# Attention and token mixing, one core: shift rows by VectorE's transposition and DRAM, and the next group's loads behind the rows of unit 2

## The reference

```
xn = layernorm(x)
q, k, v = heads(xn @ w_in.T)                  # 16 heads of 16 channels
att = where(causal, q @ k.T / 4, 0.0)         # masked scores are 0, not minus infinity
att = softmax(att)                            # so every later key has weight exp(0 - max)
a = (att @ v) @ w_out.T
x_prev = xn, one token later
r = sigmoid((mu_r * xn + (1 - mu_r) * x_prev) @ W_r.T)
k2 = square(relu((mu_k * xn + (1 - mu_k) * x_prev) @ W_k.T))
out = x + a + r * (k2 @ W_v.T)
```

## Time and profile before

| | us |
|---|---|
| median of 3 runs | 1128.43 |
| lowest, highest | 1125.78, 1129.91 |
| profiled execution, its time | 1134.35 |
| profiled execution, its span | 1132.6 |
| TensorE busy | 1080.0 (95%) |
| VectorE busy | 842.5 (74%) |
| ScalarE busy | 713.4 (63%) |
| GpSimd busy | 385.8 (34%) |
| mean granted clock of TensorE | 0.983 of full |

### The profile page before, as it was taken

How to read it: one execution, slowest core, us unless ns; L and a number is a source line. 1 busy time by engine, 2 the same in 40 slices (tenths; PEclk the granted TensorE clock), 3 DMA queues, 4 the chain that set the end, 5 groups by cost and what they waited for, 6 DMA issues and landing times.

```text
span 1132.6 us, 21906 instructions
## 1 busy us (share of the span) xinstructions
PE 1080.0 (95%) x8192; PEld 542.6 (48%) x8192; DVE 842.5 (74%) x1153; ACT 713.4 (63%) x1519; POOL 385.8 (34%) x945
## 2 busy tenths in 40 slices
PE   5999998999999999999989999999999989999998
PEld 3665554544444444444435444444444434444445
DVE  5567787678879787987867878878887878789213
ACT  2433333267776677777757776777777657767672
POOL 3211121354414341444224424442532433244301
PEclk9999999999999899999969999999999989999999
DMA  3585744392019000900280019002800460002033
GB/s 127 174 271 177 214 149 149 131 117 62 2 20 122 30 3 17 124 31 7 37 119 11 6 22 140 8 7 38 124 6 6 58 104 7 6 2 86 25 98 117
DMA packets 53390, 83.61 MB, mean 74 GB/s; under 512 B 6308, under 2 KB 36260, under 8 KB 49572
## 3 DMA queue, kind: packets, MB, share of 16 engines
q1 hardware_dynamic: 52132, 78.01, 32.9%
q0 software_dynamic: 1152, 4.19, 1.2%
HBM read 43.78 MB, written 33.55 MB: 68 GB/s over the span
## 4 chain that ended last, share of the span: by engine, by line
PE 75%; DVE 13%; ACT 4%; issue 4%; DMA 2%; POOL 0%; SPq 0%; ACTq 0%; DVEq 0%; POOLq 0%
PE ps_o L1189 22%; PE ps_s L1175 21%; DVE part_max L347 10%; PE ps_m L330 7%; PE ps_vr L733 4%; ACT probs L1039 4%; PE ps_qk L724 4%; PE ps_m L1220 3%; PE ps_o L1200 2%; PE ps_m L337 2%; PE ps_xt L782 2%; PE ps_qk L733 2%; PE ps_s L1164 2%; DMA x_in<-x 1%; PE ps_pieces L330 1%
## 5 line engine op out<-in xcount | busy, mean ns | idle before, releaser
L1039 ACT ACTIVATE probs<-ps_s 128x512 f32<-128x512 f32 (+3 forms) x1280 | 599.6, 536 | 249.6 <-PE ps_s L1175 241.5
L347 DVE TENSOR_REDUCE part_max<-ps_m 128x2 f32<-128x1024 f32 (+2 forms) x594 | 616.6, 1059 | 152.7 <-PE ps_m L330 115.1
L1175 PE MATMUL ps_s<-q_op,k_op 50*128 50x512 f32 (+3 forms) x1280 | 447.9, 429 | 10.0 <-ACT probs L1039 5.2
L330 PE MATMUL ps_m<-k_op,q_op 48*128 48x512 f32 (+3 forms) x1188 | 355.3, 419 | 16.6 <-DVE part_max L347 9.4
L1175 PEld LDWEIGHTS ps_s<-q_op,k_op 50*128 50x128 f32 x1280 | 210.7, 188 | 313.1 <-ACT probs L1039 214.2
L984 POOL TENSOR_SCALAR_AFFINE_SELECT probs<-probs 128x128 f32<-128x128 f32 x512 | 145.0, 292 | 485.7 <-ACT probs L1039 477.2
L1189 PE MATMUL ps_o<-probs,v_sb 128*32 128x512 f32 (+3 forms) x2560 | 307.9, 551 | 2.2 <-issue 2.2
L330 PEld LDWEIGHTS ps_m<-k_op,q_op 48*128 48x128 f32 x1188 | 169.3, 189 | 43.8 <-DVE part_max L347 33.8
L950 POOL TENSOR_TENSOR diag_weight<-ident,masked_weight 128x256 f32<-128x256 f32 x256 | 150.5, 623 | 40.7 <-ACT masked_weight L1005 40.7
L337 PE MATMUL ps_m<-mask,pick 64*128 64x64 bf16 (+1 forms) x932 | 96.5, 210 | 0.0
L1189 PEld LDWEIGHTS ps_o<-probs,v_sb 128*32 128x32 f32 x2560 | 51.1, 108 | 76.7 <-issue 38.1
(11 more groups left out here) (81 smaller groups left out, 715.9 us busy)
## 6 DMA issues: line engine op xcount, KB each, us to landing
parts_d<-parts SPq DMA_DIRECT2D x32, 512.0 KB, 4.7
q_op<-parts_d SPq DMA_DIRECT2D x42, 256.0 KB, 13.9
k_op<-parts_d SPq DMA_DIRECT2D x42, 256.0 KB, 16.2
vpad_d<-v_pad SPq DMA_DIRECT2D x32, 256.0 KB, 3.3
v_sb<-vpad_d SPq DMA_DIRECT2D x8, 1024.0 KB, 12.4
x_in<-x SPq DMA_DIRECT2D x8, 512.0 KB, 5.2
ffn_d<-ffn SPq DMA_DIRECT2D x8, 512.0 KB, 3.2
attn_t<-normed SPq DMA_DIRECT2D x128, 32.0 KB, 2.0
```

The costliest lines, as they stand in the source:

```text
L330: last = pe.matmul(ps_m[:, f % ring * 2 + e, 0:width], self.q_op[rows, p, j, q0:q0 + P], self.k_op[rows, p, j, pc * CH:pc * CH + width], s ...
L347: dve.tensor_reduce(both, ps_m[:, bank:bank + 2, 0:width], AX_X, ALU.max).then_inc(self.piece_reduced, 1)
L1039: act.activation(probs[:, slot % PRING, 0:width], ps_s[:, bank_of("scores", slot, first, last), 0:width], ACT.Exp).then_inc(probs_ready, 1)
L1175: pe.matmul(ps_s[:, bank_of("scores", slot, first, last), 0:CH - q0], k_op[rows, p, h % 2, kt * P:(kt + 1) * P], q_op[rows, p, h % 2, u * ...
```

## The change

TensorE's turns and ScalarE's copies go. VectorE gets a fourth step, which transposes the 128x32 tile shift in blocks of 32x32. A block then holds 32 queries of all rows, so SyncE stores the four blocks to DRAM, where the queries of a row come to lie side by side, waits for these stores, and loads the rows from there into q_op. In SyncE's queue the q and k loads of the next group move from the head of a group to behind normed of the last group's unit 3 and behind the rows of unit 2. Banks of ps_s are counted through all groups, since a group's uses are no longer a multiple of three.

```diff
-MAX_STEPS = 3
+MAX_STEPS = 4
-SHIFT_AT = {(3, 3): 0, (3, 10): 1, (1, 2): 2, (2, 8): 3}
+WEIGHT_AT = {(3, 3): 0, (3, 10): 1, (1, 2): 2, (2, 8): 3}
...
-        self.shift_t = sb("shift_t", [SHIFT_PARTS * GH, 2, CH])
+        self.shift_t = sb("shift_t", [P, 2, HW])
+        self.shift_d = nc.dram_tensor("shift_d", [2, SHIFT_PARTS, 2, GH // 2, CH], F32, kind="Internal").ap()
...
     def place_shift(self, sp, p, u, n):
         sp.wait_ge(self.shift_t_ready, n + 1)
+        sp.wait_ge(self.shift_loaded[u % 2], (n // 2 + 1) * self.SHIFTS)
+        by_block = self.shift_d[u % 2].rearrange("r e j (s b w) -> b s (r e j) w", s=SUB, w=HW)
+        for b in range(P // HW):
+            sp.dma_start(by_block[b], self.shift_t[b * HW:(b + 1) * HW, u % 2]).then_inc(self.shift_stored, 16)
+        sp.wait_ge(self.shift_stored, (n + 1) * (P // HW) * 16)
         for part in range(SHIFT_PARTS):
             for e in range(2):
-                row, at = e * HALF + ROWS + part, part * GH + e * 2
+                row = e * HALF + ROWS + part
                 sp.dma_start(self.q_op[row:row + 1, p, :, u * CH:(u + 1) * CH].bitcast(F32),
-                             self.shift_t[at:at + 2, u % 2]).then_inc(self.shift_loaded[u % 2], 16)
+                             self.shift_d[u % 2, part, e].unsqueeze(0)).then_inc(self.shift_loaded[u % 2], 16)
...
     def max_step(self, dve, k, u, n, reduced):
+        if k == 3:
+            dve.wait_ge(self.shift_ready, n + 1)
+            if n >= 2:
+                dve.wait_ge(self.shift_stored, (n - 1) * (P // HW) * 16)
+            dve.transpose(self.shift_t[:, u % 2], self.shift[:, u].rearrange("p s r h -> p (s r h)")).then_inc(self.shift_t_ready, 1)
...
             def group(i, p, first=False, last=False):
-                if not last:
-                    if not first:
-                        sp.wait_ge(scores_ready, (i * 2 + p) * SLOTS)
-                    ops.load_scores(sp, i + p, 1 - p)
                 if not first:
                     keep_normed(i - 1 + p, 1 - p, NCH - 1)
                 ops.place_shift(sp, p, 2, unit_of(i, p, 2))
                 if not last:
+                    if not first:
+                        sp.wait_ge(scores_ready, (i * 2 + p) * SLOTS)
+                    ops.load_scores(sp, i + p, 1 - p)
                     sp.wait_ge(masked_done, unit_of(i, p, 0) + 1)
                     sp.wait_ge(probs_used, weighed_to(unit_of(i, p, 0)))
                     ops.load_values(sp, i + p, 1 - p)
...
-            def turn_shift(u, n, bank):
-                pe.wait_ge(shift_ready, n + 1)
-                for s in range(SUB):
-                    last = pe.transpose(ps_s[0:SHIFT_PARTS * GH, bank, s * P:(s + 1) * P],
-                                        shift[:, u, s].rearrange("p r h -> p (r h)"), ident[:])
-                last.then_inc(shift_turned, 1)
...
-            def keep_shift(u, n, earlier, bank):
-                act.wait_ge(shift_turned, n + 1)
-                act.wait_ge(shift_loaded[u % 2], (earlier + 1) * SHIFTS)
-                act.copy(shift_t[:, u % 2], ps_s[0:SHIFT_PARTS * GH, bank]).then_inc(shift_t_ready, 1)
```

More of the change, by code:

```diff
@@ L120, in score_uses, with bank_of @@
                 uses.append(("suffix", SV_AT[u, kt]))
-            if (u, kt) in SHIFT_AT and not (u == NCH - 1 and last):
-                uses.append(("shift", SHIFT_AT[u, kt]))
             uses += [("scores", (KT0[u] + kt) * GH + at) for at in range(GH // 2, GH)]
     return uses
-def bank_of(what, which, first, last):
-    return (score_uses(first, last).index((what, which)) + 2 * first) % SRING
+def bank_of(what, which, G):
+    first, last = G == 0, G == B * NG - 1
+    before = sum(len(score_uses(g == 0, False)) for g in range(G))
+    return (before + score_uses(first, last).index((what, which))) % SRING
 def rows_of(h, rows):
@@ L676, in batch @@
                     high_part(n, par, 1)
-                    if (n, 0) in TOKEN_SHIFT_AT:
-                        keep_shift(TOKEN_SHIFT_AT[n, 0])
                     act.wait_ge(v_stored[par], stores * (SUB * 16) + CREDIT)
@@ L735, in two_tiles @@
                 return last
[L737 to L742, removed]
-                for s in range(SUB):
-                    last = pe.transpose(ps_m[0:SHIFT_PARTS * GH, 0, s * P:(s + 1) * P],
-                                        ops.shift[:, u, s].rearrange("p r h -> p (r h)"), ident[:])
-                last.then_inc(ops.shift_turned, 1)
             def batch(b, last_batch):
@@ L1039, in group @@
                             act.activation(probs[:, slot % PRING, 0:width],
-                                           ps_s[:, bank_of("scores", slot, first, last), 0:width], ACT.Exp).then_inc(probs_ready, 1)
+                                           ps_s[:, bank_of("scores", slot, i * 2 + p), 0:width], ACT.Exp).then_inc(probs_ready, 1)
                             if h != GH // 2 - 1:
@@ L1044, in group @@
                                 keep_suffix(0, FIRST_SV_AT[u, kt], FIRST_SV_AT[u, kt],
-                                            bank_of("own suffix", FIRST_SV_AT[u, kt], first, last))
+                                            bank_of("own suffix", FIRST_SV_AT[u, kt], i * 2 + p))
                             if (u, kt) in SV_AT and not last:
                                 keep_suffix(1 - p, SV_AT[u, kt], (G + 1) * 4 + SV_AT[u, kt],
[L1048 to L1053, removed]
+                                            bank_of("suffix", SV_AT[u, kt], i * 2 + p))
+                            if (u, kt) in WEIGHT_AT and not (nxt and last):
+                                weight(unit_of(i, p, WEIGHT_AT[u, kt] + nxt), WEIGHT_AT[u, kt])
                         if kt == LAG - 1 and not (first and u == 0):
@@ L1143, in wait_for_bank @@
                     pe.wait_ge(v_after_ready, uses[at][1] + 1)
-                elif uses[at][0] == "suffix":
+                else:
                     pe.wait_ge(v_after_ready, (G + 1) * 4 + uses[at][1] + 1)
-                else:
-                    pe.wait_ge(shift_t_ready, unit_of(i, p, uses[at][1] + (NCH if uses[at][1] < 2 else 0)) + 1)
-            def turn_shift(u, n, bank):
-                pe.wait_ge(shift_ready, n + 1)
-                for s in range(SUB):
-                    last = pe.transpose(ps_s[0:SHIFT_PARTS * GH, bank, s * P:(s + 1) * P],
-                                        shift[:, u, s].rearrange("p r h -> p (r h)"), ident[:])
-                last.then_inc(shift_turned, 1)
             def sum_suffix(p, quad, n, bank):
@@ L1174, in score_tile @@
                 wait_for_bank("scores", slot, i, p, first, last)
-                pe.matmul(ps_s[:, bank_of("scores", slot, first, last), 0:CH - q0], k_op[rows, p, h % 2, kt * P:(kt + 1) * P],
+                pe.matmul(ps_s[:, bank_of("scores", slot, i * 2 + p), 0:CH - q0], k_op[rows, p, h % 2, kt * P:(kt + 1) * P],
                           q_op[rows, p, h % 2, u * CH + q0:(u + 1) * CH], start=True, stop=True).then_inc(scores_ready, 1)
@@ L1235, in between_scores @@
                     wait_for_bank("own suffix", FIRST_SV_AT[u, kt], i, p, first, last)
-                    sum_suffix(0, FIRST_SV_AT[u, kt], 0, bank_of("own suffix", FIRST_SV_AT[u, kt], first, last))
+                    sum_suffix(0, FIRST_SV_AT[u, kt], 0, bank_of("own suffix", FIRST_SV_AT[u, kt], i * 2 + p))
                 if (u, kt) in SV_AT and not last:
                     wait_for_bank("suffix", SV_AT[u, kt], i, p, first, last)
[L1239 to L1243, removed]
+                    sum_suffix(1 - p, SV_AT[u, kt], G + 1, bank_of("suffix", SV_AT[u, kt], i * 2 + p))
             def group(i, p, first=False, last=False):
```

19 lines of the change are left out of this document (4 added, 15 removed).

## The result

The changed kernel takes 1174.51 us in the median (1171.6 to 1184.73, 4 runs), against 1129.17 us for the kernel before beside it. The ratio is 1.0418, with a 95% interval of 1.0346 to 1.0490. The forecast was 1178 us. The profiled execution took 1184.73 us. All ratios are formed from fast runs, those within 1.5% of the fastest of their kernel, which leaves runs out in one place: eight of the ten of ahead20_pool in experiment 8.

A forecast was written before the change was run, and what follows sets the result against it. TensorE bounds the kernel, and its waits for data are lost in full. 1134.35 + 49.6 (groups 1 to 6) - 1.4 (group 0) - 1.5 (group 7) - 3.0 (token stage) = 1178 us; range 1148 to 1208 us.

The forecast's parts named there:

- The bound and the step that decides: TensorE at tile 17 waits for all twelve q and k loads, which the move makes late; chance of the stop 0.83.
- The ladder: SyncE's queue, step by step from a group's start: normed, row stores, row loads, then big loads at 24.3, landed at 54.3 us.
- the stores' round trip: Unit 2's four row stores to DRAM and the wait for their landing: 4.6 us, bounds 2.5 and 6.5.
- The loads' 30 us: The twelve q and k loads, 3 MB set by busy DMA engines, take 30.0 us from first issue to last landing.
- The stop: TensorE stands still at tile 17 for some 10.9 us in each of groups 1 to 6.
- the turn of unit 2: Removing unit 2's four TensorE transpositions brings TensorE to tile 17 1.0 us earlier; measured before as 0.95 us.
- The clock: Half clock behind each stop in groups 1 to 6: 10.24 us of work, costing 3.4 us a group, bounds 0 and 6.8.
- The last group: Group 7 loads nothing and loses two turns: -1.5 us.
- The rival that the loads come in time: TensorE would not stop at tile 17 and only the removals show: 1111 us, or nearer 1119; chance 0.07.
- The rival of a second wait: Slow row stores on SyncE also delay rows of unit 3 or the next group's units: 1220 us or more; chance 0.08.
- 4 us in hand: GpSimd adds up late-landing values till 65 us, then masks tile 20, which TensorE wants at 69 us or later.
- theory A3: Follow-up forecast for split48: loads in flight slow the instruction fetch, so split's stops go; 1093 to 1100 us.

The follow-up runs named there:

- ahead20_pool: Changed kernel with the next group's pieces begun at tile 20, not 17, and GpSimd adding up next values behind masking unit 2's diagonal; 1141.33 us, median of ten.
- experiment 8: Changed kernel with next pieces begun at tile 20, not 17, and GpSimd's adding of next values moved behind masking unit 2's diagonal; ratio 0.9925 (0.9874 to 0.9975).
- experiments 3, 4, 5: In order: split; rows_first; and the changed kernel with only six of twelve q and k loads from group 2's operands on, 1095.62 us.
- before_moved: Experiment 2: the kernel before, its turns kept, with only the q and k loads moved behind normed and the rows of unit 2; 1179.12 us.
- turns_back: rows_first with TensorE's four transpositions per unit and ScalarE's copy put back, into a tile nobody reads; 1111.65 us.
- rows_first: Changed kernel with the rows of unit 2 first, then all twelve q and k loads, then normed of the last group's unit 3; 1095.32 us.
- after_pool: Changed kernel with only GpSimd's order changed: the next group's values added up behind masking unit 2's diagonal; 1172.97 us.
- split: Changed kernel with six of the twelve q and k loads at the head of a group, six behind the rows of unit 2; 1108.14 us.
- split48: split with four q and k loads at the head of a group and eight behind the rows of unit 2; 1098.34 us.

## Why the prediction was right, point by point

**The bound and the step that decides** were right: TensorE waits for all twelve loads ahead of the first new piece, and the move makes them late. Undoing the lateness in three ways (experiments 3, 4, 5) took away the loss each time; making the loads late without the rest of the change (experiment 2) brought the loss.

**The ladder.** Forecast and measured, in us into a group: normed issued 14.7 and 14.5, stores 17.2 and 17.1, row loads 21.8 and 20.8, loads 24.3 and 23.2, landed 54.3 and 53.9 in group 3. The one rung that was off is the stores' round trip: 592.62 - 588.88 = 3.7 us, where I took 4.6 from normed's transfers of eight times the size. The loads' 30 us held: 595.00 to 625.7 us. By the Trainium skill, page "DMA: Bandwidth & Descriptors", section "Anatomy of one DMA — SWDGE (gpsimd) path", whose fit is for another issue path, they would be an estimate of 9 us; the trace does not agree, in this kernel or in any of the others. Each of these loads writes 16 partitions; whether that sets their rate, no run here tried.

**The stop** was forecast at 10.9 us and is 9.8 us at the most, 9.2 on average (55.3 / 6). The loads land 0.4 to 1.5 us sooner than forecast (0.9 on average), and TensorE's last matmul ahead of the wait ends 44.2 us into a group, 0.8 later than the 43.4 that I had. Part of this is the turn of unit 2, which I counted at 1.0 us: the piece runs 44.2 us into most groups of turns_back and 43.7 into those of rows_first, so the turn is worth about 0.5. Nearly half of that gap on TensorE was no loss. VectorE was nearly full at the head of the group (first stretch), but that it took up the other half isn't shown.

**The clock** was at half behind all six stops. I took 10.24 us of work at half clock; here it is between 5.9 and 16.5 us, 11.6 on average. Two of these stretches of the changed kernel, then the starts of groups 1 and 7 in rows_first, in before_moved and in turns_back:

```profile
744.20:760.70 16.50, 16.46 (x95) 8.38 (x95) 7.26 (x10) 8.32 (x16) 5.96 (x19) 0.50 0.16 52
987.00:992.80 5.80, 5.80 (x36) 3.32 (x37) 2.18 (x4) 2.52 (x5) 2.41 (x8) 0.50 0.32 102
...
333.00 0.50 PE L1138 MATMUL ps_s<-q_op,k_op 50*128 50x512 f32 x1
...
968.00 0.50 PE L1138 MATMUL ps_s<-q_op,k_op 50*128 50x512 f32 x1
...
346.17 0.50 PE L1173 MATMUL ps_s<-q_op,k_op 50*128 50x512 f32 x1
...
1045.24 0.50 PE L1173 MATMUL ps_s<-q_op,k_op 50*128 50x512 f32 x1
...
333.97 0.50 PE L1148 MATMUL ps_s<-q_op,k_op 50*128 50x512 f32 x1
...
980.94 0.50 PE L1148 MATMUL ps_s<-q_op,k_op 50*128 50x512 f32 x1
```

On average over these six groups, one of the changed kernel, with 9.2 us of stop, is 13.9 us longer than one of rows_first, and one of before_moved, with 4.8 us of stop, 8.7 us longer than one of turns_back. So 4.7 and 3.9 us a group are left for the clock, against 3.4 forecast.

**The sum.** Groups 1 to 6 take 1050.96 - 332.56 = 718.4 us against 718.2 forecast, as the shorter stop and the dearer half clock cancel. That it fits to 0.2 us is luck: in after_pool, with much the same stops (53.7 us in all), they take 711.0 us. In the profiled executions these groups make +49.8 us. Group 0 gave 2.0 us (1.4 forecast) and the token stage 3.5 (3.0). VectorE's transposition takes 203 ns, where I took 0.2 us between the two of the earlier trace rows. The last group was off in that execution: 4.8 us longer, not 1.5 shorter, with 13.66 us at half clock behind no stop of that length. Together that is +49.1 us of span. The last group is part of why the profiled run lies 10 us above the median; its groups 1 to 6, longer than after_pool's, are likely to be another. What sets off the half clock in the last group I didn't find. Between the medians the change costs 45.3 us, where the forecast's terms add up to 43.7.

**The rival that the loads come in time** was wrong for the change. Its price, 1111 us, is near what split measured (1108), where the loads do come in time, but two of its terms were off: split has two stops that the price left out, and the turns are worth 14 to 16 us, not 20. It was too dear for rows_first. I had kept the idle stretches without a releaser, as at 572.80 us in the earlier trace rows, and the half clock behind them, as part of the kernel. In rows_first the granted clock is 1.000 over the whole run.

**The rival of a second wait** named SyncE's rows as its place, and nothing waited for them. The second wait that did lie behind the first was GpSimd's, which I had weighed and dismissed as 4 us in hand. That was true of the changed kernel (after_pool), and not of the kernel with the first wait mended.

## What to carry to other kernels

When a transfer is moved behind others in one queue, add up the queue to the landing, and compare that with the first instruction that wants the data: here 15 us of slack against 24 us of move decided the outcome. Ask of each transfer in the queue what its own wait is: the rows of unit 2 were ready at 7 us and stood behind normed, ready at 14.5 us, and putting the rows, with the loads behind them, ahead of normed turned a loss of 4.2% into a gain of 3.2%. And slack that is counted behind a stall is not slack once the stall is mended.

## What the runs showed that I had not expected

**A stop that nothing in the profile releases.** The stops of 3.00 us before the change and of 2.85 us in split each begin 0.4 to 0.8 us after a fetch of 16 KB on the instruction queue starts. Such a fetch took 1.7 to 2.0 us there, against a median near 0.9 us outside the loads. That TensorE ran out of instructions would fit, but it is not shown, and some rows speak against the simple form of it. The first line is the stretch of split's stop in group 6, as above; the second, from the table of DMA queues, is the instruction queue in split from 668.8 to 671.3 us, in group 4 (fetches, MB, share of 16 engines):

```profile
880.85:883.70 2.85, 0.00 (x1) 0.00 (x0) 1.09 (x2) 0.16 (x1) 0.81 (x2) 1.00 0.07 14
...
q8 instruction: 1, 0.02, 4.7%
```

In the stop the DMA engines are nearly idle (0.07). And 4.7% of 16 engines in 2.5 us is a fetch of 1.9 us at the same place of group 4, without a stop; groups 2 and 3 of split have one of 1.7 to 1.8 us there, and no stop either. In split48, too, a fetch near 8 us into groups 1 and 3 to 6 took 1.8 to 1.9 us, beside the first four loads, and no stop followed. So theory A3's forecast came true, but not by a quicker fetch. Moving the loads off that moment removed the stops (split48, rows_first); by what way stays open.

**Half clock cost nearly as much behind a short stop as behind a long one.** Beyond the stop itself a group lost 3.9 us behind 4.8 us of standing still (before_moved), 4.7 us behind 9.2 (the changed kernel), and some 3 us behind 2.5 (split, group 1: 111.74 us against 106.00 in split48). Of the work at half clock that is 0.43, 0.40 and 0.3, where the prediction took a third from the earlier trace rows.
